# Newton steps on another engine, a first store on another queue, and biases added in one tile: a two-layer FFN and attention kernel

## The reference, cut to what matters

```python
def _layernorm(x, axis=-1, eps=1e-05):
    m = jnp.mean(x, axis=axis, keepdims=True)
    v = jnp.var(x, axis=axis, keepdims=True)
    return (x - m) / jnp.sqrt(v + eps)
...
    def _L0_attn_ref(x, Wq, bq, Wk, bk, Wv, bv, Wo, bo):
...
        q = split_heads(x @ Wq.T + bq)
        k = split_heads(x @ Wk.T + bk)
        v = split_heads(x @ Wv.T + bv)
...
        attn = jax.nn.softmax(scores, axis=-1)
        ctx = jnp.einsum('bhqk,bhkd->bhqd', attn, v)
...
        return ctx @ Wo.T + bo
...
        weights = _golden_weights(x, Wr, temperature)
        gate = jnp.einsum('btd,edf->betf', x, Wg)
        up = jnp.einsum('btd,edf->betf', x, Wu)
        h = jax.nn.silu(gate) * up
        e_out = jnp.einsum('betf,efd->betd', h, Wd)
        out = jnp.einsum('bte,betd->btd', weights, e_out)
...
    x = x + 0.5 * _L0_ffn_ref(_layernorm(x, axis=-1), ...)
    x = x + _L0_attn_ref(_layernorm(x, axis=-1), ...)
    x = x + 0.5 * _L0_ffn_ref(_layernorm(x, axis=-1), ...)
```

## Time and profile before

| what | us |
|---|---|
| median of 3 runs | 884.58 |
| lowest, highest | 883.81, 886.05 |
| the profiled execution | 883.35 |
| its span, first to last instruction | 881.6 |
| PE busy | 792.5 |
| DVE busy | 508.9 |
| POOL busy | 383.7 |
| ACT busy | 344.4 |

### The profile page before, as it was taken

How to read it: one execution, slowest core, us unless ns; L and a number is a source line. 1 busy time by engine, 2 the same in 40 slices (tenths; PEclk the granted TensorE clock), 3 DMA queues, 4 the chain that set the end, 5 groups by cost and what they waited for, 6 DMA issues and landing times.

```text
span 881.6 us, 13749 instructions
## 1 busy us (share of the span) xinstructions
PE 792.5 (90%) x4856; PEld 617.4 (70%) x4856; DVE 508.9 (58%) x1424; ACT 344.4 (39%) x656; POOL 383.7 (44%) x365
## 2 busy tenths in 40 slices
PE   3397897989988999979999897899999999999997
PEld 3286786857656676667767666677667677888886
DVE  5367677485666753586754466855446743475332
ACT  3134334424355343244533335444325344232321
POOL 3064564236432453242344334245344455446664
PEclk9889899999999999998999999999999999999999
DMA  4534433514412422221252213234222223222331
GB/s 155 168 108 144 120 109 96 140 53 108 106 58 77 121 74 86 60 72 55 84 151 73 73 55 90 73 109 108 94 76 73 74 73 96 72 72 80 125 108 49
DMA packets 60617, 81.93 MB, mean 93 GB/s; under 512 B 8066, under 2 KB 44162, under 8 KB 60548
## 3 DMA queue, kind: packets, MB, share of 16 engines
q1 hardware_dynamic: 58816, 80.90, 30.5%
q10 hardware_dynamic: 1732, 0.15, 0.1%
HBM read 68.17 MB, written 12.71 MB: 92 GB/s over the span
## 4 chain that ended last, share of the span: by engine, by line
PE 66%; DVE 21%; issue 3%; ACT 3%; DMA 3%; SPq 2%; POOL 1%; POOLq 0%; DVEq 0%; ACTq 0%
PE gu L408 10%; PE gu L410 10%; PE gu L409 10%; PE dn L427 5%; PE dn L428 5%; PE dn L429 5%; PE ra L517 4%; PE ra L490 4%; PE ra L505 3%; DVE junk L856 3%; PE ra L385 2%; DVE hid L821 2%; DVE hid L814 2%; PE ra L481 2%; SPq L992 1%
## 5 line engine op out<-in xcount | busy, mean ns | idle before, releaser
L912 POOL TENSOR_TENSOR hid<-hid,wb 128x512 f32<-128x512 f32 x128 | 167.7, 1311 | 299.0 <-DVE hid L821 267.0
L408 PE MATMUL gu<-xt_hi,wgu_hi 128*128 128x512 f32 x512 | 232.4, 454 | 16.6 <-DVE hid L814 16.6
L916 POOL TENSOR_TENSOR ht_lo<-hid,ht_hi 128x512 fp32r<-128x512 f32 x128 | 165.6, 1293 | 159.1 <-ACT ht_hi L619 159.0
L856 DVE CUSTOM_DVE_ANT_0 junk<-ra,mask 128x128 bf16<-128x128 f32 (+3 forms) x256 | 124.0, 488 | 161.0 <-PE ra L490 159.7
L410 PE MATMUL gu<-xt_lo,wgu_hi 128*128 128x512 f32 x512 | 206.1, 403 | 0.0
L409 PE MATMUL gu<-xt_hi,wgu_lo 128*128 128x512 f32 x512 | 204.9, 400 | 0.0
L427 PE MATMUL dn<-wd,ht_hi 128*128 128x256 f32 x512 | 164.8, 322 | 1.3 <-POOL ht_lo L916 1.3
L664 ACT ACTIVATE probs<-ra 128x512 f32<-128x512 f32 x160 | 95.4, 597 | 171.6 <-PE ra L505 170.9
L814 DVE SCALAR_TENSOR_TENSOR hid<-hid,gu 128x512 f32<-128x512 f32 x128 | 87.6, 684 | 122.4 <-ACT hid L612 121.9
L619 ACT ACTIVATE ht_hi<-hid 128x512 fp32r<-128x512 f32 x128 | 80.4, 628 | 187.9 <-POOL hid L912 166.9
L428 PE MATMUL dn<-wd,ht_hi 128*128 128x256 f32 x512 | 145.7, 285 | 0.0
(11 more groups left out here) (126 smaller groups left out, 859.2 us busy)
## 6 DMA issues: line engine op xcount, KB each, us to landing
wd<-wd_parts SPq DMA_DIRECT2D x56, 512.0 KB, 3.5
wb<-wts_rows SPq DMA_DIRECT2D x64, 256.0 KB, 3.9
qk_parts<-parts SPq DMA_DIRECT2D x32, 192.0 KB, 2.1
q_st<-qk_parts SPq DMA_DIRECT2D x96, 64.0 KB, 3.3
k_st<-qk_parts SPq DMA_DIRECT2D x96, 64.0 KB, 2.5
wd_parts<-wd SPq DMA_DIRECT2D x8, 512.0 KB, 5.1
x_res<-in_x SPq DMA_DIRECT2D x4, 512.0 KB, 6.5
stage<-in_Wg SPq DMA_DIRECT2D x8, 256.0 KB, 3.9
```

The costliest lines, as they stand in the source:

```text
L408: mm(b_, w_hi, xt_hi[q % 2][:, c, :], start=c == 0, stop=False)
L856: nc.vector.tensor_tensor_reduce(out=junk[:, USE[it] % NA, 0:w], in0=o[:, 0:w], in1=mask[:, T - w:T], scale=1.0, scalar=-3.0e38, op0=ALU.a ...
L912: nc.gpsimd.tensor_tensor(tb, tb, wb[m % NWB][:, :], ALU.mult).then_inc(hw_done, 1)
L916: nc.gpsimd.tensor_tensor(ht_lo[n % NHT][:, :], hid[n % NHID][:, :], f32(ht_hi[n % NHT][:, :]), ALU.subtract).then_inc(lo_done, 1)
```

## The change

- `rstd_piece` is gone. DVE takes the statistics (`stats`), eps and first guess (`var`); POOL makes the three Newton steps, of four instructions each, and the shift (`newton`, in two items, 12 + 2 instructions). The statistics of batches 1, 2 and 3 for the first layer are taken together, 12 tiles at once, in chunks 3 to 5. There are 10 sets instead of 12.
- The routing weights of block 0 are stored by ACT, directly behind its copy to `wt`, and ACT also issues the first two loads of `wb`. SP issues the loads of x for batches 2 and 3 together.
- The two-row matmuls of `v` and `wo` are gone. One tile `bias_all` is made once in chunk 17 (item `bias`: bv times Wo plus bo, since the softmax rows sum to one), and POOL adds it to `x_res` after the attention's `xn` has been made from it (`xb`).
- The rows of -1.0 in `k_st` are set by two DMAs from a small tile `minus` of 96 partitions instead of a memset of 2 partitions.
- PE signals when the first two row tiles of a block are complete, DVE's first addition waits for that alone, and SP stores each half of a batch by itself.
- Routing is cut in eight pieces; the split of the first expert's Wg and Wu comes before `small`.

```diff
@@ schedule @@
-        put(2 * e - 3.0 if e else -8.6, ("sg", e))
+        put(2 * e - 3.0 if e else -9.45, ("sg", e))
...
-    for b, t in enumerate((-21, -6.0, -1.0, 3.0)):
+    for b, t in enumerate((-21, -6.0, 0.9, 1.8)):
...
+    put(17.8, ("bias",))
...
+    for j in range(6):
+        put(3.6 + 0.2 * j, ("stats", 1, j))
+    put(4.9, ("var", 1))
+    put(5.1, ("newton", 1, 0))
+    put(5.4, ("newton", 1, 1))
@@ tensor: v and wo, bias, d @@
-                            mm(b_, ones[:, :], rows[:, w - 2, :], start=True, stop=False)
...
+                        if k == CB - 1 and i == 1:
+                            last.then_inc(half_done, 1)
...
+                    if kind == "bias":
+                        pe.wait_ge(bv_done, 2)
+                        pe.wait_ge(a_lo, 2)
+                        for c in range(KT):
+                            w_hi, w_lo = wa[:, 3, c, 0:D], wa[:, 3, c, D:2 * D]
+                            mm(o[:, 0:D], bv_hi[:, c, :], w_hi, start=c == 0, stop=False)
+                            mm(o[:, 0:D], bv_hi[:, c, :], w_lo, start=False, stop=False)
+                            last = mm(o[:, 0:D], bv_lo[:, c, :], w_hi, start=False, stop=c == KT - 1)
@@ scalar @@
+                act.dma_start(bias_all[:, :], A["bo"]).then_inc(small_in, 16)
...
-                        act.wait_ge(small_in, 80)
+                        act.wait_ge(small_in, 96)
...
+                        for c in range(2):
+                            act.dma_start(k_st[KROWS + c:KROWS + c + 1, :, :, :].rearrange("a s h t -> a (s h t)"),
+                                          minus[48 * c:48 * (c + 1), :]).then_inc(minus_in, 16)
...
+                        if q == 0:
+                            act.wait_ge(*emptied(it))
+                            act.dma_start(wts_dram[q].rearrange("e i t -> (e i) t"), wt[:, :]).then_inc(w_st, 16)
+                    if kind == "wb" and it[1] < NWB:
+                        m = it[1]
+                        act.wait_ge(w_st, 16)
+                        act.dma_start(wb[m][:, :], wts_dram[0, m].rearrange("i t -> (i t)").unsqueeze(0).to_broadcast([P, T])
+                                      ).then_inc(wb_ld[m], 16)
@@ vector @@
-                def rstd_piece(b, k):
...
+                    if kind == "bias":
+                        dve.wait_ge(bv_done, 1)
+                        for c in range(KT):
+                            ins = nc.vector.tensor_scalar(bv_lo[:, c, :], f32(bv_hi[:, c, :]), -1.0, bv[:, c:c + 1], ALU.mult,
+                                                          ALU.add)
+                        ins.then_inc(bv_done, 1)
+                        dve.wait_ge(ra_full, full(it))
+                        nc.vector.tensor_tensor(bias_all[:, :], o[:, 0:D], bias_all[:, :], ALU.add).then_inc(freed, 1)
...
+                            dve.wait_ge(*((half_done, q + 1) if m == 0 else (down_done, CB * (q + 1))))
@@ gpsimd @@
-                chain(nc.gpsimd.memset(k_st[KROWS:SROWS, :, :, :], -1.0))
+                chain(nc.gpsimd.memset(minus[:, :], -1.0))
...
+                    if kind == "newton":
+                        k, half = it[1:]
+                        tile = slice(STATS_OF[k][0] * QT, STATS_OF[k][1] * QT)
+                        y, v, tmp = rstd[:, tile], var[:, tile], ntmp[:, tile]
+                        pool.wait_ge(var_done, VAR_DONE[k])
+                        for _ in range((2, 1)[half]):
+                            link(nc.gpsimd.tensor_tensor(tmp, y, v, ALU.mult))
+                            link(nc.gpsimd.tensor_tensor(tmp, tmp, y, ALU.mult))
+                            link(nc.gpsimd.tensor_scalar(tmp, tmp, -0.5, 1.5, ALU.mult, ALU.add))
+                            link(nc.gpsimd.tensor_tensor(y, tmp, y, ALU.mult))
+                        if half == 1:
+                            link(nc.gpsimd.tensor_tensor(tmp, mv[:, tile, 0], y, ALU.mult))
+                            nc.gpsimd.tensor_scalar(shift[:, tile], tmp, -1.0, None, ALU.mult).then_inc(st_done, 1)
+                    if kind == "xb":
+                        b, m = it[1:]
+                        xt = x_res[:, b * QT + 2 * m:b * QT + 2 * m + 2, :]
+                        pool.wait_ge(aln_done, 2 * (2 * b + m + 1))
+                        pool.wait_ge(*emptied(("bias",)))
+                        nc.gpsimd.tensor_tensor(xt, xt, bias_all[:, :].unsqueeze(1).to_broadcast([P, 2, D]),
+                                                ALU.add).then_inc(xb_done, 1)
@@ sync @@
-                        sp.wait_ge(x_done, 2 * q + 2)
-                        sp.dma_start(out[b * T:(b + 1) * T, :].rearrange("(i p) d -> p i d", p=P),
-                                     x_res[:, b * QT:(b + 1) * QT, :]).then_inc(out_sem, 16)
+                        for m in range(2):
+                            sp.wait_ge(x_done, 2 * q + m + 1)
+                            sp.dma_start(out[b * T + m * HT:b * T + (m + 1) * HT, :].rearrange("(i p) d -> p i d", p=P),
+                                         x_res[:, b * QT + 2 * m:b * QT + 2 * m + 2, :]).then_inc(out_sem, 16)
```

More of the change, by code:

```diff
@@ L51 @@
 MASKS = 3
-CONSTS = 9
-ROUTE_PIECES = 5
-RSTD_PIECES = 4
+CONSTS = 7
+ROUTE_PIECES = 8
+NEWTON = 3
+STATS_OF = [(0, 1), (1, BATCH)] + 2 * [(b, b + 1) for b in range(BATCH)]
 def f32(ap):
@@ L138, in schedule @@
         head = meet[0] - (9.8 if b else 7.65)
-        for k in range(RSTD_PIECES):
-            put(head - 1.4 + 0.25 * k, ("arstd", b, k))
+        s = BATCH + 2 + b
+        put(head - 1.4, ("stats", s, 0))
+        put(head - 1.2, ("stats", s, 1))
+        put(head - 1.1, ("var", s))
+        put(head - 0.95, ("newton", s, 0))
+        put(head - 0.7, ("newton", s, 1))
+        for m in range(2):
+            put(head + 3.0 + 2.0 * m, ("xb", b, m))
         put(head - 0.4, ("aln", b, 0))
@@ L224, in build @@
         USE = {it: k for k, it in enumerate(it for it in PE_ORDER if it[0] in RING)}
+        ends = [it[1] for it in POOL_ORDER if it[0] == "newton" and it[2] == 1]
+        STATS_DONE = {("ln", q): ends.index(min(q, 1) if q < BATCH else q - BATCH + 2) + 1 for q in range(NBLOCK)}
+        STATS_DONE |= {("aln", b): ends.index(BATCH + 2 + b) + 1 for b in range(BATCH)}
+        VAR_DONE = {it[1]: k + 1 for k, it in enumerate(it for it in DVE_ORDER if it[0] == "var")}
         XN_BEFORE, latest = {}, {}
@@ L241, in build @@
         bk = sb("bk", [P, KT])
-        rows = sb("rows", [2, 2, D], F32R)
-        ones = sb("ones", [2, P], F32R)
-        sel = sb("sel", [2, 1])
+        bv = sb("bv", [P, KT])
+        bias_all = sb("bias_all", [P, D])
         ident = sb("ident", [P, P])
@@ L1027 @@
         "bk": np.ascontiguousarray(raw("attn_bk").reshape(KT, P).T),
[L1028 removed]
+        "bv": np.ascontiguousarray(raw("attn_bv").reshape(KT, P).T),
+        "bo": row("attn_bo"),
     }
```

163 lines of the change are left out of this document (81 added, 82 removed), and 2 rows, old and new, of the table DELAY.

## The result

The kernel before took 884.19 us in the runs beside the changed one (median of 4, 882.88 to 886.05), the changed kernel 852.16 us (median of 4, 850.41 to 853.12). The ratio is 0.9634, with a 95% interval of 0.961 to 0.9658. The forecast was 854.5 us with a range of 840 to 873, and faster with a chance of 0.91. The profiled execution took 851.86 us, its span 850.1 us.

A forecast was written before the change was run, and what follows sets the result against it. PE, busy 792.5 of 881.6 us, was taken as the bound, so gains need fewer matmuls, less standing still or shorter ends. Terms summed to -30.1 us: 883.35 became 853.3, plus 1.2 gives 854.5 us, range 840 to 873.

The forecast's parts named there:

- Part 1: Start chain: storing the first routing weights from ScalarE's queue makes store and wb load land sooner, a gain of 6.3 us.
- rival (b): Two-row matmuls were cheap as PE would wait anyway; store gains only issue time, wb 4 us slower: 868.5 us; shared chance 0.22.
- Part 2: Start up to the first xn: shorter memset, but 14 dependent POOL instructions at 0.25 us; +0.4 us (-1 to +2.5).
- Part 3: Newton steps moved from DVE to POOL: PE's stops beside them and low clock afterwards shrink, -14 us (-26 to -3).
- five places: Five PE stops beside Newton steps after 100 us, 14.4 us together, plus some 12 us lost to the lower clock.
- Rival (d): POOL becomes the bound in each Newton stretch; at 0.6 us per small instruction the kernel is slower, 910 us; chance 0.05.
- Part 4: v and wo tiles: dropping 32 two-row matmuls of 0.5 us frees 16 us of PE, counted as -12 (-16 to -6).
- Part 5: Chunks 3 to 5: statistics of three batches at once load DVE, +2 us (0 to 4); same work saved later under cover.
- Part 6: Kernel end: last rows added and stored by halves, the second half ending sooner, -0.9 us (-1.4 to -0.4).

## Why the prediction was right, and where its steps were not

The total was 2.3 us off and the range held. That it is so close is partly luck: several terms were off, by up to 6 us, in both directions.

| term | forecast us | measured us | from |
|---|---|---|---|
| store on ACT's queue | -6.3 | -3.1 | store on SP again |
| first xn | +0.4 | +0.85 | xn at 12.62 and 11.77 |
| Newton steps off DVE | -14 | -8.1 | Newton steps on DVE again |
| two-row matmuls | -12 | -16.1 | before without them |
| bias item | +0.7 | +2.9, without its matmuls | bias operands earlier |
| statistics together | +2 | +0.5 | all statistics apart |
| last rows by halves | -0.9 | -1.3 | time from PE's last matmul to the end |
| sum | -30.1 | -24.4 | whole change: -32.0 |

- **Part 1.** The issue wait went as said, and the store landed in 2.46 us, sooner than my 3.3. The failed step is the load of wb: between 3.55 and 7.6 us "I take 4.8, since it has a queue of its own". It took 7.6, the upper end, and over 8 with the loads of x out of its way. A queue of its own gave it no share at first: it moved nothing for 3 us, while SP's transfers went on, and then shared the engines. Nor does the store show that a queue of its own passes others. It was issued at 27.63, when one load of 256 KB had gone out on SP 0.08 us before it, and not at 31.99 behind 2 MB that had not landed; the run with the store on SP moves the time of issue and the queue together, so which of the two gave 2.46 instead of 5.8 us stays open. The Trainium skill, "DMA: Bandwidth & Descriptors", section "Issuing engines are not separate DMA queues", says that issuing on several engines saves only the time to issue; the 7.6 us of wb agree with it, and no run here tests it with the store. The half of rival (b) that had wb slower by 4 us came true (7.6 against 3.55 us), but the store landed sooner than it had.
- **Part 2.** The interval of 0.28 us (I had 0.25) and one instruction held for 1.24 us, as allowed for. ACT waited for the output bias until 10.33, but xn was released by shift.
- **Part 3.** The direction and the held DVE instruction were right. Two steps failed. First, the size: 8.1 us. Second, where it comes from. I expected stops to go; I had named an idle time still near 50 us after 60 us as a sign that I was wrong, and the stops longer than 0.3 us after 50 us do sum to 47.6 us with the change (47.9 with the steps back on DVE, 53.2 before). So this sign of being wrong came true for Part 3. What changed is that most stops of 2.5 to 3.7 us became shorter ones (six stops over 2.5 us with DVE's steps, one with POOL's), and PE kept 2.4 GHz, above all in chunks 50 to 56. I had counted five places; 8.6 of the 11.4 us between the two profiles come from this one.
- **Part 3, POOL's side.** "POOL idles for more than half" was right and no comfort. Rival (d) was priced by POOL's free time per chunk, with 2.8 us of slack at each place. The run with six steps shows under 1 us: 30 us more chain brought 23 us of idle time and cost 36.8 us with the clock, and two steps instead of three gave back 8.0 us over ten sets. So rival (d) named the right danger by the wrong mechanism: what decides is the length of the chain (14 times 0.28 us, and 4.87 us in the mean with what stands between), not POOL's load. DVE's chain of three steps took 4.12 us, so the move paid a part of its gain for the longer one.
- **Part 4.** The 0.5 us for each matmul was exact, and my discount for waits (16 to 12) was wrong: PE's idle time stayed at 88.3 us, so nothing that had been hidden behind these matmuls came out. The bias item cost more than its matmuls, because bv_lo was placed behind two hid products.
- **Part 5.** My +2 at chunk 12 was near the 2.9 us measured, and the late saving, which I had called "under cover", is worth most of it back.
- **Part 6.** 1.3 us, inside my ends, by the traces alone; no run undid it.

The measured terms leave 7.7 us of the 32.0 unexplained. They need not add, as the undo runs each have their own stretches at the lower clock (47.6 us in all in the profiled execution before, 24.9 with the change), and one of them is an edit of the kernel before. The routing in eight pieces, the rows of -1.0 by DMA and the earlier split of the first weights were not tried by themselves, so this stays open.

## What to carry to other kernels

A half-idle engine can still be on the path: read the length of its dependent chain at the place where its result is wanted, not its load, and test it by making the chain longer. PE's idle time and its clock are two accounts; with the same idle time, a few stops of 3 us instead of more of 1 to 2 us went with 8 to 10 us more here, most of it in one place: look there first. Where two traces show a gain vanish by some point, undo one part alone before calling it given back: here another part's cost had covered it.

## What the runs showed of the hardware

- One matmul with two rows of operands cost 0.5 us for 256 columns, where six full ones take 0.68 to 0.70 us. All 16 us of 32 such matmuls came off the time.
- Small POOL instructions of 4 or 12 columns last 0.20 us, 0.28 us from start to start. DVE's 1.23 us subtraction held one of them for 1.24 us, just as POOL's product holds one of DVE's.
- On DVE the first, second and third instruction of a Newton step averaged 272, 381 and 163 ns over 30, with the steps back on DVE: the first two were held now and then, up to 1.28 us, the third never (in the kernel before, once in 36). Of POOL's 130 three lasted over 0.5 us.
- A 16 KB store landed in 2.46 us when it was issued on ACT's queue 0.08 us after the first of a row of weight loads, and in 5.8 us on SP's queue behind 2 MB of them. A 256 KB load on ACT's queue, issued in the middle of the row, moved nothing for 3 us and landed after 7.6 us.
- The stop behind xt_lo near 375 us: 3.1 us or more went with 10.2 to 13.7 us at 1.2 GHz in four traces, 1.6 us with none in seven. Near 517 us the same stop of 2.5 us was followed by 3.4 us in one trace and by 13.7 us in another.
